# Row-wide maxima, 16-bit contexts and paced key loads in a cross-attention layer on one core

## The reference, cut to what matters

```python
# cross-attention: hidden_q = layernorm(x), kv_c = ctx_512 (2, 4096, 128)
q_hk = (hidden_q @ Wq.T).reshape(B, S, H, K)
q_big = apply_rope(einsum('bshk,hkq->bshq', q_hk, w_kc_q))      # 384 wide
kv_r = apply_rope(kv_c)
q_r = einsum('bshq,hqr->bhsr', q_big, W_qr)
k_r = einsum('bld,hdr->bhlr', kv_r, W_kr)
attn = softmax(einsum('bhsr,bhlr->bhsl', q_r, k_r))
ctx_c = einsum('bhsl,bld->bhsd', attn, kv_r)                    # 128 wide
ctx = einsum('bhsd,hkd->bhsk', ctx_c, w_kc_kv)                  # then @ Wo.T
x = x + ctx @ Wo.T
# mixing: scores over the heads of one token, no softmax
x = x + (einsum('bnhk,bnkd->bnhd', q k^T, v)) @ Wo              # q, k, v from layernorm(x)
# feed-forward: silu(gate) * up, then down; weights are integers less 128, scaled
x = x + ffn(layernorm(x))
```

## Time and profile before

| | |
|---|---|
| Median of 3 runs | 1070.21 us (1066.58 to 1074.66) |
| The profiled execution, own time | 1078.67 us |
| its span, first to last instruction | 1076.9 us |
| TensorE busy | 1031.6 us, 96% |
| VectorE, ScalarE, GpSimd busy | 863.0, 759.1, 622.9 us |
| mean granted TensorE clock | 0.986 |

### The profile page before, as it was taken

How to read it: one execution, slowest core, us unless ns; L and a number is a source line. 1 busy time by engine, 2 the same in 40 slices (tenths; PEclk the granted TensorE clock), 3 DMA queues, 4 the chain that set the end, 5 groups by cost and what they waited for, 6 DMA issues and landing times.

```text
span 1076.9 us, 24647 instructions
## 1 busy us (share of the span) xinstructions
PE 1031.6 (96%) x9456; PEld 724.3 (67%) x9456; DVE 863.0 (80%) x1241; ACT 759.1 (70%) x1188; POOL 622.9 (58%) x812
## 2 busy tenths in 40 slices
PE   6789998999999999999999999999999999999988
PEld 4344544766766677777777777777777745768877
DVE  5799887989999999999998999999999604544633
ACT  2133338888888899989998999999999631426532
POOL 1983352788888877768777777777776412000000
PEclk9899999999999999999999999999999999998999
DMA  9443365999999999999999999999999960050000
GB/s 366 131 157 107 105 141 100 195 196 205 205 203 199 211 205 202 203 199 207 205 203 193 195 211 204 199 207 197 196 202 194 219 253 5 1 203 23 1 21 20
DMA packets 568933, 180.15 MB, mean 167 GB/s; under 512 B 551536, under 2 KB 557680, under 8 KB 568176
## 3 DMA queue, kind: packets, MB, share of 16 engines
q1 hardware_dynamic: 567456, 173.86, 76.9%
q10 hardware_dynamic: 1360, 4.72, 1.1%
HBM read 39.07 MB, written 1.05 MB: 37 GB/s over the span
## 4 chain that ended last, share of the span: by engine, by line
PE 83%; DMA 8%; DVE 5%; ACT 2%; issue 1%; POOLq 1%; SPq 0%; POOL 0%; ACTq 0%; DVEq 0%
PE ps_o L1316 10%; PE ps_o L1317 10%; PE ps_o L1320 10%; PE ps_s L1297 6%; PE ps_s L1299 6%; PE ps_s L1298 6%; DMA pt_both<-p_both 5%; PE ps_o L1377 5%; PE ps_t L1297 3%; PE ps_t L1298 3%; PE ps_t L1299 3%; PE ps_t L1217 2%; DMA kvr<-ctx_kv_dram 2%; PE ps_s L1194 1%; DVE wq_lo L875 1%; PE ps_s L1467 1%
## 5 line engine op out<-in xcount | busy, mean ns | idle before, releaser
L989 DVE SCALAR_TENSOR_TENSOR p_both<-prob,p_both 128x1024 f16<-128x1024 f32 x256 | 325.9, 1273 | 38.0 <-ACT p_both L674 33.1
L682 ACT ACTIVATE prob<-sized,nmax 128x1024 f32<-128x1024 f32 x256 | 293.3, 1146 | 28.7 <-DVE sized L1000 25.8
L674 ACT ACTIVATE p_both<-prob 128x1024 f16<-128x1024 f32 x256 | 270.6, 1057 | 34.3 <-DMA pt_both<-p_both 12.2
L1316 PE MATMUL ps_o<-kn,pt_both 128*128 128x128 f16 x2048 | 258.2, 220 | 11.2 <-DMA pt_both<-p_both 10.9
L1317 PE MATMUL ps_o<-kn,pt_both 128*128 128x128 f16 x2048 | 258.2, 220 | 0.0
L1316 PEld LDWEIGHTS ps_o<-kn,pt_both 128*128 128x128 f16 x2048 | 200.9, 98 | 47.8 <-DMA pt_both<-p_both 11.7
L1000 DVE TENSOR_SCALAR_CACHE_REDUCE sized<-ps_s,against 128x1024 f32<-128x1024 f32 x170 | 217.2, 1278 | 9.4 <-PE ps_s L1299 3.9
L1317 PEld LDWEIGHTS ps_o<-kn,pt_both 128*128 128x128 f16 x2048 | 201.4, 98 | 27.1
L1320 PE MATMUL ps_o<-kn,pt_both 128*128 128x128 f16 x2048 | 157.0, 220 | 0.0
L544 POOL TENSOR_TENSOR oscl<-ocopy,weigh 128x512 f32<-128x512 f32 x64 | 94.7, 1480 | 85.2 <-ACT ocopy L696 82.4
L1297 PE MATMUL ps_s<-kt,q_hi 128*128 128x512 f16 x340 | 128.9, 379 | 1.3 <-DVE qcos L907 1.3
(11 more groups left out here) (214 smaller groups left out, 1786.0 us busy)
## 6 DMA issues: line engine op xcount, KB each, us to landing
wgu_raw<-w_gu_dram SPq DMA_DIRECT2D x11, 512.0 KB, 9.9
wq_s<-wq_t_dram SPq DMA_DIRECT2D x16, 256.0 KB, 3.8
wot_s<-wo_t_dram SPq DMA_DIRECT2D x16, 256.0 KB, 2.8
kvr<-ctx_kv_dram ACTq DMA_DIRECT2D x4, 1024.0 KB, 12.7
pt_both<-p_both SPq DMA_TRANSPOSE x256, 4.0
kvr<-w_mix_dram SPq DMA_DIRECT2D x4, 1024.0 KB, 9.2
wkcq_s<-w_kcq_dram SPq DMA_DIRECT2D x16, 192.0 KB, 2.5
wdn_raw<-w_dn_dram SPq DMA_DIRECT2D x1, 2816.0 KB, 8.9
```

The lines of the kernel that those rows point to most:

```text
L674: nc.scalar.mul(p_hi(n), prob[:, n % 2, :], PSCALE).then_inc(hi_done, 1)
L682: nc.scalar.activation(prob[:, n % 2, :], sized[:, n % 2, :], ACT.Exp, bias=nmax[:, i, c:c + 1], scale=-1.0, accum_out=rsum[:, i, c:c + 1] ...
L989: nc.vector.scalar_tensor_tensor(out=p_lo(n), in0=prob[:, n % 2, :], scalar=PSCALE, in1=p_hi(n), op0=ALU.mult, op1=ALU.subtract).then_inc( ...
L1316: nc.tensor.matmul(o, pt_hi[:, k, :], kn[:, b, p, 0, keys], start=(k == 0), stop=False)
```

## The change

Five things are changed.

1. *Key loads.* The four key transfers of ScalarE's queue are gone; SP loads each piece's 512 columns of keys with that piece's tables in `load_turn`, and the second piece is moved behind `load_wq(2)`.
2. *Row maximum.* The exponentials of a row are all taken on the row's maximum (`nrow`). VectorE runs `FIRST` = 5 chunks ahead with maxima, TensorE `AHEAD` = 9 with scores, `sized` has six buffers. All four chunks are then added up by TensorE in the same 128 columns of PSUM; `weights_of_chunks`, `take_chunks`, `chunk_weights` and `sum_chunks` are gone. GpSimd keeps the sum and its inverse (`row_sum`).
3. *Contexts.* ScalarE scales the row's context and rounds it to 16 bits (`take_context`), VectorE takes the lower half (`context_low`), and every eighth chunk SP turns two rows' halves by one transfer of four blocks (`turn_contexts`).
4. *Output weights.* ScalarE sums their absolute values (`size_weights`, 16 activations) for a power of two, and GpSimd splits them in rows 16 to 31 (`split_weights`).
5. *Behind the loop.* A head's context product is three 16-bit products of 128x512. Tile 0's are placed in the last eight chunks of the loop (`DRAIN`); tile 2's are cut in two around the turned norms; the mixing weights are split one load at a time.

The last queries are also absorbed ahead of the first exponential, where they stood behind the first two.

```diff
-AHEAD = 5
+AHEAD = 9
+FIRST = 5
+KEPT = 6
+DRAIN = 8
...
             def load_turn(p, i):
                 for m, src in ((0, cos_k), (1, sin_k)):
                     sp.dma_start(cs_k[:, i, m, :], src[:, bass.ds(p * PIECE, PIECE)]).then_inc(cs_in[i], 16)
+                cols = slice(p * PIECE, (p + 1) * PIECE)
+                sp.dma_start(kvr[:, :, cols], kv_v[:, :, cols]).then_inc(cs_in[i], 16)
...
+            def turn_contexts(p):
+                sp.wait_ge(ctx_done, 2 * (p + 1))
+                sp.dma_start(ctx16[:, 2 * p:2 * p + 2].rearrange("d t a q -> d (t a) q"),
+                             c_both[:, p % 2].rearrange("q t a d -> q (t a d)"), transpose=True)\
+                  .then_inc(ctx_in[p % 2], 16)
...
             for n in range(NCHUNK):
                 turn_exponents(n)
-                if n % 8 == 6 and 1 <= n // 8 <= NP:
+                if n % 8 == 2 and 1 <= n // 8 <= NP:
                     turn_keys(1, n // 8 - 1, kt_next)
+                if n % 8 == 6 and n >= 8:
+                    turn_contexts(n // 8 - 1)
...
             sp.wait_ge(pv_done, NCHUNK)
-            for m in range(4):
+            load_mix(0)
+            turn_contexts(NQT // 2 - 1)
+            for m in range(1, 4):
...
             for t in range(NQT):                                  # GpSimd
-                if t + 2 < NQT:
-                    split_query(t + 2)
-                if t:
-                    sum_chunks(t - 1)
-                chunk_weights(t)
+                if t + 3 < NQT:
+                    split_query(t + 3)
+                row_sum(t)
                 if t % 2 and t // 2 < NP:
                     split_keys(1, t // 2)
+                if 2 * NP <= t < 2 * NP + H:
+                    split_weights(t - 2 * NP)
...
+            def size_weights(p):                                  # ScalarE
+                act.wait_ge(d_ok, 2 * p + 2)
+                act.wait_ge(qsum_ok, 2 * p + 2)
+                for h in (2 * p, 2 * p + 1):
+                    if h:
+                        act.wait_ge(wsum_ok, h)
+                    nc.scalar.activation(q_size[:, :], wo_abs[:, h * D:(h + 1) * D], ACT.Abs,
+                                         accum_out=qsum[:, H + h:H + h + 1]).then_inc(wsum_ok, 1)
...
                 take_qabs(p)
+                if p:
+                    size_weights(p - 1)
...
             def exponents(n):
-                act.wait_ge(m_done, n + 1)
+                i, c, t = n // NCH % 2, n % NCH, n // NCH
+                act.wait_ge(nrow_done, t + 1)
...
+            def take_context(t):
+                act.wait_ge(pv_done, NCH * (t + 1))
+                act.wait_ge(lrec_ok, t + 1)
...
+                nc.scalar.mul(c_both[:, p % 2, t % TPH, 0, :], ps_o[:, t % 2, 0:P],
+                              lrec[:, t % 2, :]).then_inc(ctx_half, 1)
...
             for n in range(NCHUNK):
                 exponents(n)
                 take_hi(n)
...
+                if n % NCH == 0 and n >= 2 * NCH:
+                    take_context(n // NCH - 2)
...
             for n in range(NCHUNK):                               # VectorE
-                if n + 1 < NCHUNK:
-                    chunk_maximum(n + 1)
+                if n + FIRST < NCHUNK:
+                    look_ahead(n + FIRST)
+                if n % NCH == 1 and n >= 2 * NCH:
+                    context_low(n // NCH - 2)
                 take_lo(n)
...
+                nc.tensor.matmul(o, ctx16[:, n, 0, :], wo16[:, h, 0, :], start=(h == 0), stop=False)
+                nc.tensor.matmul(o, ctx16[:, n, 0, :], wo16[:, h, 1, :], start=False, stop=False)
+                last = nc.tensor.matmul(o, ctx16[:, n, 1, :], wo16[:, h, 0, :], start=False, stop=(h == H - 1))
```

More of the change, by code:

```diff
@@ L379, in refill @@
                 load_wq(h + 2, i)
+                if h == 0:
+                    load_turn(1, 1)
+                    load_rotated(1)
                 sp.wait_ge(b_done, QC * (h + 1))
@@ L539, in sum_chunks @@
[L539 to L546 removed]
+                                        ALU.mult).then_inc(lsum_ok, 1)
```

358 lines of the change are left out of this document (182 added, 176 removed).

## The result

The changed kernel took **1056.85 us** (median of 4 runs, 1052.96 to 1059.17), the kernel before 1072.43 (4 runs, 1066.58 to 1078.48): ratio 0.9861, 95% interval 0.9819 to 0.9902. The profiled execution took 1059.17 us (span 1057.4), the one before 1078.7 (span 1076.9).

What follows compares the result with a forecast made beforehand. TensorE was taken as the bound nearly everywhere, GpSimd in the stretch up to 367 us. Terms -6 + 6 - 2.2 + 2 - 33 = -33 us took 1078.7 to 1045.5, from the median 1037 us; range 1019 to 1057.

Steps and rivals of the forecast that it cites:

- the loop without gaps: Loop: TensorE has no gap after about 200 us, and the loop ends at 857.4 against 859.6, -2.2 us.
- 422/455 = 93% full becomes 95%: VectorE in the loop: one more 128-column operation a row, estimated 0.3 us of 10.5, still leaves it cover.
- Transfers, "+2": In-order transfer queue: 31 small context turnings join it and cost +2 us, between nothing and 19.
- Rival 1: Transfer queue is full (12%): blocks of keys and contexts exceed its rate in the loop, +19 us, 1056.
- the 0.93 per eight chunks goes: Early loop: without the `weigh_ok` wait, GpSimd's 22.0 us per eight chunks falls under TensorE's 21.1, removing 0.93 each.
- -6 + 6: Preparation: paced key loads gain 6 us, and 16 activations sizing the output weights cost 6 us.
- 1.5 us were said: Preparation: VectorE idles about 1.5 us before `wq_lo` at three boundaries, because of the sizes.
- The ramp: Loop's start: exponential 0 starts at 174.1 us and weighed products 4 can start at 196.0.
- Behind the loop, "-33": After the loop: cheaper context products and tile 2 cut in two gain 33 us, between 25 and 36.
- Rival 5: Change does nothing in the loop (2%): GpSimd's 22.0 us stays, `split_weights` adds 16 such rows, +8 +8, 1053.
- Rivals 3 and 4: 3: everything covered (12%), -45, 1025. 4: slower (4%), `take_context` waits expose part of a transfer each row, 1127.
- rival 2: Preparation and weights cost more (17%): sizes 8 us, pacing gains 3, -25 behind the loop: -20, 1050.

Runs made afterwards that it cites:

- the steps apart and a fourth buffer: Changed kernel with four buffers for rounded exponentials and the output weights' splitting given out one step a row over rows 16 to 59: 1043.9 us, ratio 0.9751.
- the fourth buffer: Changed kernel with four buffers for the rounded exponentials in place of three: 1050.8 us, ratio 0.9807.
- contexts twice: Changed kernel with each transfer of context halves issued a second time, into a buffer nobody reads: 1080.6 us, ratio 1.0063.
- before, fourth buffer: Kernel before with four buffers for the rounded exponentials in place of three: 1073.3 us, ratio 1.0015.
- loads at once: Changed kernel with the key loads of the kernel before, four loads of 1 MB issued at once by ScalarE: 1055.2 us, ratio 0.9864.
- tile 0 behind: Kernel with all helpful edits together (1033.1 us), but tile 0's 48 context products after the loop, not in its last eight chunks: 1040.0 us, ratio 0.9714.

## Why the prediction was wrong

**The step that failed** is the loop without gaps, and in it first "422/455 = 93% full becomes 95%. That is the closest cover here; if it fails, the price is small". By it the loop was to end at 857.4; the changed kernel got there near 877, and the 20 us between them are the stalls, 11.1 in rows 0 to 15 and 9.0 in rows 16 to 31. For rows 16 to 31 the mechanism was wrong. The share was a mean over 390 to 845 us of the kernel before, a stretch in which GpSimd does no 512-column splitting. `split_weights` was checked against GpSimd's own room only, and there it fits. What it does to VectorE was not priced: 1.35 us in each of 16 rows, on an engine with 0.4 us to spare a row. Its row then takes 11.15 us to TensorE's 10.54, 9.8 us over 16 rows by that estimate. The measured price is 9.0 us, shown twice: it moves with the splitting, and with the steps apart and a fourth buffer it falls to 0.3.

It could have been had from the kernel before, by looking at how long a low half lasts beside each GpSimd step of the key splitting, not at its mean of 1273 ns. Beside the multiplication that starts at 332.17, and beside the subtraction of the same piece:

```profile
332.67 1.62 DVE L989 SCALAR_TENSOR_TENSOR p_both<-prob,p_both 128x1024 f16<-128x1024 f32 x1
...
335.48 1.68 DVE L989 SCALAR_TENSOR_TENSOR p_both<-prob,p_both 128x1024 f16<-128x1024 f32 x1
```

The first begins 0.50 us behind the multiplication and again ends 1.08 us behind its end. The busy share would not have told it: VectorE is at 93% in the stretch with key splitting too, 144.68 of 155 us, where only every second row has these steps.

**Transfers, "+2".** Too small, and the reason given for it too easy. The first rows hold 11.1 us of stalls, and the fourth buffer took 4.8 of them: there the ring of three closes. That it does so when keys and contexts stand ahead of an exponentials' transfer is argued from the queue's order, not shown. Rival 1 had the time, 1056, and part of the place, but not the mechanism: 9.0 of the 20 us are VectorE's, and the queue moves 140 blocks per eight chunks without a stall once there is a fourth buffer. That a small transfer can be dear it had right, as "contexts twice" shows. The transfers of the changed kernel (count, median us from issue to landing):

```profile
pt_both<-p_both SPq DMA_TRANSPOSE x256, 3.9
kvr<-w_mix_dram SPq DMA_DIRECT2D x4, 1024.0 KB, 7.7
...
ctx<-c_both SPq DMA_TRANSPOSE x32, 2.6
kt<-kn SPq DMA_TRANSPOSE x16, 3.0
```

A quarter of the blocks takes two thirds of the time to land (2.6 against 3.9), which the earlier trace rows half showed: 3.4 for half the blocks.

**Rows 0 to 15, "the 0.93 per eight chunks goes".** GpSimd's 22.0 us were read rightly (before, fourth buffer: still 22.0, ratio 1.0015), and without `weigh_ok` GpSimd can keep 21.1, as the changed kernel with a fourth buffer shows. But the change as it stands brought these rows no gain, 11.4 us of stalls before and 11.1 after: another limit, the ring of three, stood right behind the one removed.

**Preparation, "-6 + 6".** The sum was right (+2.0 in the profiled pair, -3.7 to +2.0 over the kernels with both), each term too small: alone, pacing is worth 9.1, and the sizes cost 5.3 to 11. The mechanism of the sizes is as forecast, VectorE idle ahead of its low half at the boundaries:

```profile
87.20 0.69 DVE L896 TENSOR_TENSOR wq_lo<-wq_s,wq_hi 128x512 fp32r<-128x512 f32 x1 [2.90 <-ACT wq_hi L616]
...
114.39 0.69 DVE L896 TENSOR_TENSOR wq_lo<-wq_s,wq_hi 128x512 fp32r<-128x512 f32 x1 [2.17 <-ACT wq_hi L616]
...
132.44 1.33 DVE L896 TENSOR_TENSOR wq_lo<-wq_s,wq_hi 128x512 fp32r<-128x512 f32 x1 [2.30 <-ACT wq_hi L616]
```

1.5 us were said. Why the pair does not add was not foreseen, and is in part open. TensorE's granted clock goes along with it: before, it is 0.90 in the window of 25 to 60 us; in the changed kernel 0.91 from 60 to 100, where TensorE waited 3.2 us; in the kernel with loads at once and sizes 1.00 in both. But no run holds the clock fixed. Between profiles with 1.00 in both windows the sizes cost 5.6 us (155.3 to 160.9 at the earliest), and pacing gains only 2.0 beside them (162.9 to 160.9); what it would gain without them at a clock of 1.00, no run shows.

**The ramp.** Weighed products 4 were to start at 196.0. TensorE in order of time has them at 195.49, so the new order of the row maximum costs about what was worked out. That it fits to 0.5 us is luck: exponential 0 began at 175.68 and not at 174.1, and the terms behind it were 2.1 us too large together.

```profile
195.49 0.22 PE L1367 MATMUL ps_o<-kn,pt_both 128*128 128x128 f16 x1
...
900.41 0.39 PE L1461 MATMUL ps_t<-nT_hi,wmix_hi 128*128 128x256 f32 x1 [1.40 <-DVE nT_lo L1135]
```

**Behind the loop, "-33".** Right. From the last weighed products to the end, fourteen kernels with the change (all but "tile 0 behind") take 180 to 186 us, mean 182.9, and four of the old form 212 to 218, mean 216.1: -33.2. The kernel before alone gave 217.5 and 211.7 in two profiles, so a single pair tells this to some 6 us. The first mixing product starts 23 us behind the loop's end of 877, said were 21.6, and 25 behind the last weighed one, said were about 22; the mixing weights land in 7.7 us and are not waited for.

**The rivals.** Rival 5, at 2%, had the amounts and the places: +8 for the stalls of before that stay and +8 for the 16 rows of `split_weights`, where 11.1 and 9.0 came. Its mechanism did not come: from 390 to 560 us GpSimd is busy for 105 of 170, and it is VectorE that its steps hold up. Rivals 3 and 4 (a ring through the contexts, at 1127) did not come. Of rival 2's terms, pacing 3 and -25 behind the loop were wrong; its 8 for the sizes lies within the 5.3 to 11 measured. The time of 1056.85 lies within the range only at its upper edge, which rivals 1 and 5 had set by mechanisms that were not at work: that is luck.

## What to carry to other kernels

When work is given to an engine with room, price it also on its neighbour: the room of the engine that executes it is not the only cover it uses. Take the durations of the tightest engine's steps from where the moved work already runs beside them, sorted by what runs beside, not by mean. Wide steps of a helper that hold up a full engine are better spread over many rows, as here. When one limit is removed, look for the one right behind it. Two edits that each shift when an engine idles are to be measured alone and together before either is called worthless.

## What the runs showed of the hardware

- VectorE's 1024-column step with two tensors, 1.21 us, becomes 2.02 when begun 0.10 us behind a 512-column GpSimd step with two tensors, and 1.62 when begun 0.50 us behind: both end 1.08 us behind the 1.04 us of that step. Behind one with one tensor and a scalar, which itself takes 1.57 us, it becomes 1.68.
- 32 transfers of four 128x128 blocks, needed by nobody, cost 24 us with buffers of three and four, 16 with four and four, 13 with four and five.
- The same preparation reached the first maximum between 160.9 and 166.6 us in ten profiles. The granted clock from 60 to 100 us was 1.00 in four of them (160.9, 161.7, 161.9 and 163.9), 0.96 in five (163.9 to 164.9) and 0.91 in the latest. A difference of 5 us there is not an edit's without a second profile.
